# The looped turns of two attentions, written out in place of loops on the engines

## The reference

```python
def reference(...):
    x = x + _L0_attn_ref(_layernorm(x), ...)   # pre-norm attention with RoPE, then a dense FFN 128-512-128
    x = x + _L0_ffn_ref(_layernorm(x), ...)    # 16 experts, top 2, gates from a softmax, relu
    x = x + _L1_attn_ref(_layernorm(x), ...)   # causal attention, plus a bias from "lines" with decay
    x = x + _L1_ffn_ref(_layernorm(x), ...)    # 8 experts, top 2, gelu
    return x
```

## Time and profile before

| | us |
|---|---|
| median of 3 runs | 2036.21 |
| lowest, highest run | 2025.66, 2040.84 |
| the profiled execution as a run | 2023.77 |
| its span in the profile | 2022.0 |

### The profile page before, as it was taken

How to read it: one execution, slowest core, us unless ns; L and a number is a source line. 1 busy time by engine, 2 the same in 40 slices (tenths; PEclk the granted TensorE clock), 3 DMA queues, 4 the chain that set the end, 5 groups by cost and what they waited for, 6 DMA issues and landing times. The chain is left out here.

```text
span 2022.0 us, 39979 instructions
## 1 busy us (share of the span) xinstructions
PE 1540.8 (76%) x11726; PEld 971.8 (48%) x11726; DVE 1276.1 (63%) x3485; ACT 891.2 (44%) x1807; POOL 681.4 (34%) x774
## 2 busy tenths in 40 slices
PE   1699989889899861999246898798888978324993
PEld 0133433334333330999124566566665756323993
DVE  1577878777787622555515686877777867453555
ACT  0156646555455530565132555445545534102552
POOL 2211222332222213455263343334433310474552
PEclk9989989979799875899558999999999999656997
DMA  4211011110111050222324434443343340411225
GB/s 106 63 52 46 30 51 53 35 60 24 50 52 46 13 190 20 65 73 68 109 74 135 123 110 124 120 135 115 107 146 107 115 129 31 121 45 50 72 69 148
DMA packets 121565, 165.67 MB, mean 82 GB/s; under 512 B 21459, under 2 KB 94963, under 8 KB 120787
## 3 DMA queue, kind: packets, MB, share of 16 engines
q1 hardware_dynamic: 112530, 145.69, 24.4%
q0 software_dynamic: 8896, 18.30, 2.6%
HBM read 116.04 MB, written 47.60 MB: 81 GB/s over the span
## 5 line engine op out<-in xcount | busy, mean ns | idle before, releaser
L943 DVE TENSOR_REDUCE a_M<-a_F 128x1 f32<-128x512 f32 x512 | 326.1, 680 | 87.4 <-PE a_F L1115 68.3
L840 ACT ACTIVATE L_W<-a_ST 128x512 f32<-128x512 f32 x512 | 277.3, 594 | 163.7 <-PE a_ST L1155 159.7
L1738 ACT ACTIVATE c_PT<-c_ST 128x1024 f32<-128x1024 f32 x160 | 163.2, 1020 | 197.1 <-PE c_ST L2045 154.4
L1155 PE MATMUL a_ST<-L_W 74*128 74x512 bf16 x512 | 179.5, 415 | 30.1 <-ACT L_W L840 14.0
L1115 PE MATMUL a_F<-L_W 72*128 72x512 bf16 x512 | 178.6, 425 | 16.1 <-DVE a_M L943 15.7
L2044 PE MATMUL c_ST<-ident,c_SD 128*128 128x128 f32 x512 | 144.1, 281 | 26.9 <-issue 17.3
L1134 PE MATMUL a_PV<-L_W,a_V 128*32 128x512 f32 x1024 | 154.9, 681 | 1.0 <-ACT L_W L840 1.0
L1155 PEld LDWEIGHTS a_ST<-L_W 74*128 74x128 bf16 x512 | 46.1, 102 | 183.3 <-ACT L_W L840 96.2
L2269 ACT ACTIVATE L_hT<-L_P,L_W1s 128x128 f32<-128x128 f32 x316 | 90.3, 368 | 98.5 <-issue 51.3
L1845 DVE TENSOR_TENSOR c_inc<-c_INC,c_table 128x512 f32<-128x512 f32 x128 | 87.5, 684 | 50.0 <-PE c_INC L2012 41.8
L2257 POOL DMA_INDIRECT L_yd<-L_ys,L_di x79 | 86.4, 1094 | 89.4 <-issue 55.9
(11 more groups left out here) (367 smaller groups left out, 3646.0 us busy)
## 6 DMA issues: line engine op xcount, KB each, us to landing
c_QS<-c_q SPq DMA_DIRECT2D x32, 504.0 KB
c_QS<-c_rd SPq DMA_DIRECT2D x32, 378.0 KB
L_xg<-L_xd SPq DMA_DIRECT2D x150, 64.5 KB
L_W<-a_q SPq DMA_DIRECT2D x32, 288.0 KB
L_W<-a_k SPq DMA_DIRECT2D x96, 96.0 KB
c_KS<-c_k SPq DMA_DIRECT2D x96, 96.0 KB
L_W<-in_L_w SPq DMA_DIRECT2D x8, 1024.0 KB, 13.3
L_got<-L_yd SPq DMA_DIRECT2D x32, 256.0 KB, 4.4
```

The costliest lines, as they stand in the source:

```text
L840: act.activation(PT[:, j, kk, :], ST[:, kk, :], ACT.Exp).then_inc(sem(exped), 1)
L943: dve.tensor_reduce(M[:, t, h:h + 1], FB[n % BANKS][:, :], AX_X, ALU.max).then_inc(sem(maxed), 1)
L1155: pe.matmul(ST[:, kk, :], KS[0:KR0, h, kt * P:(kt + 1) * P], QS[0:KR0, h, :], start=True, stop=True).then_inc(sem(scored), 1)
L1738: act.activation(PT[:, j, :, :], ST[:, :, :], ACT.Exp).then_inc(sem(exped), 1)
```

## The change

The three loops become Python loops: the body is emitted once for every turn, with i a number. The order of the pieces in a turn, the buffers and the semaphores stay as they are.

```diff
--- before.py
+++ after.py
@@ -579,7 +579,7 @@
             before = ("projected", 1, 3)
             run(0, False, True, True, False, order_of(False, True, True, False, before))
             run(1, True, True, True, False, order_of(True, True, True, False, before))
-            with eng.Fori(2, B - 2) as i:
+            for i in range(2, B - 2):
                 run(i, True, True, True, True, order_of(True, True, True, True, before))
             run(B - 2, True, True, False, True, order_of(True, True, False, True, before))
             run(B - 1, True, False, False, True, order_of(True, False, False, True, ("ffn", -2, 0)))
@@ -1370,7 +1370,7 @@
         def turns(eng, run):
 
             run(0, False, True, True, order_of(False, True, True, (NEXT[-1][0], 1, NEXT[-1][2])))
-            with eng.Fori(1, B - 2) as i:
+            for i in range(1, B - 2):
                 run(i, True, True, True, order_of(True, True, True, ("pv", -1, NQ - 1)))
             run(B - 2, True, True, False, order_of(True, True, False, ("pv", -1, NQ - 1)))
             run(B - 1, True, False, False, order_of(True, False, False, ("pv", -1, NQ - 1)))
@@ -1611,7 +1611,7 @@
             prep(0, first=True)
             shape_table()
             prep(1)
-            with pool.Fori(2, B) as i:
+            for i in range(2, B):
                 bias_tokens(i - 2)
                 prep(i)
             bias_tokens(B - 2)
```

## The result

The changed kernel takes 2021.7 us at the median (2005.92 to 2029.05, 17 runs); beside it the kernel before took 2038.26 us (2023.01 to 2047.61, 17 runs). The ratio is 0.9929, 95% interval 0.9907 to 0.9951: 0.7% faster. That is inside the range of the prediction and within 1%, but it is a gain where 2 us of loss were forecast.

What follows compares the result with a forecast made beforehand. The prediction took looped turns to be bound by TensorE and its exchanges with ScalarE and VectorE, in the second attention also by transfers. Terms -0.3 - 1.0 + 3.0 + 0.3 = +2.0 us on 2036.2 gave 2038 us, range 2020 to 2056.

Steps and rivals of the forecast that it cites:

- Back edges: Loop ends of both attentions: hidden in the first, saving 0; four in the second at 0.08 us save 0.3 us.
- Register instructions: Semaphore targets computed in looped turns: 0.11 us each where one holds a wait, one per turn on the path, saving 1.0 us.
- Instruction fetching: Written-out turns must be fetched: turns 2 to 5 of the second attention lose 3.0 us, the first attention 0.3 us.
- The clock: First attention's turns 2 to 5: tiny shifts move the clock's falls, gain of 8 or loss of 11 us; 22 in 100.
- The faster rival: Both attentions: TensorE's waiting register instructions all on the path, 17.3 us saved, 2019 us; 9 in 100 with the other faster rival.
- The 3 in 100 for a saving of fetches at the back edges: Second faster rival, at the loops' back edges: writing out saves instruction fetches there; 3 in 100.
- The slower rival: Mainly second attention: fetches delay many awaited transfers, 0.80 us each, up to 56 us; 11 in 100.

Runs made afterwards that it cites:

- the fast place: The follow-up runs beside which the unchanged kernel before took 1989 and 1988 us, where other follow-up runs had it at 2021 to 2024 us.
- rest_out: Kernel before with the turns of all engines but TensorE written out in both attentions; ratio 0.9929 to the kernel before.
- pe_out: Kernel before with only TensorE's turns written out in both attentions, other engines looped; ratio 1.0014 to the kernel before.
- swap_loops: Kernel before, loops kept, ScalarE's two waits ahead of each exponential in exchanged order; ratio 0.9997 to the kernel before.
- more_reg: Kernel before, loops kept, one more register target and wait for ScalarE ahead of each exponential in looped turns; ratio 0.9988 to the kernel before.
- one_turn_loops: Changed kernel with each written-out turn inside a loop of one pass, entry and branch kept; ratio 0.9906 to the kernel before.
- one_turn_2: Repeat of one_turn_loops, the changed kernel with each written-out turn in a loop of one pass; ratio 0.9861 to the kernel before.
- first_only: Kernel before with only the first attention's loop written out; ratio 0.9992 to the kernel before.
- second_only: Kernel before with only the second attention's loops written out, the common one and GpSimd's own; ratio 0.9988 to the kernel before.

## Why the prediction was wrong

**Back edges (-0.3 us).** Mis-sized. The pair of the earlier trace rows compared a back edge (4.52) with a loop's entry (4.44), and both carry loop work. Against the written-out boundary of 4.20 us, the entry costs 0.24, four back edges 0.32 each and the exit 0.09: 1.6 us. The first attention's 0 was right, its last two steps keep 3.70 us in all turns.

**Register instructions (-1.0 us).** Right in kind, too small and on the wrong engine. I counted TensorE's; the runs put most of the price on the other engines, the fixed steps on ScalarE and VectorE, which stand between TensorE's results and its next operands. The fixed steps are 4 x 0.18 and 5 x 0.22, together 1.8 us. "0.11 us each, one per turn" missed that the first attention has three such places and the second three.

**Instruction fetching (+3.3 us).** This is the step that failed and turned the sign of the sum. The packets came (36 in four turns), the delay did not. I had one fetched turn, in which ScalarE waited 1.78 us before line 1671, and made it the price of every fetched turn. In the eight profiles in which all turns are written out or stand in loops of one turn, 40 turns moved 8 to 10 instruction packets each and the wait was 0.95 to 0.98 us in all of them. It was over 1 us in 12 turns of the other profiles (up to 2.64 us), ten of them turn 1, all with 8 to 10 packets; in turns without packets it was never over 0.99 us. So a fetch may still be part of that delay in some programs, and what else it takes is open. I had written "the rows show the coincidence, not the cause" and priced it nonetheless. In the changed kernel the wait was 0.96 us against 0.98, so there the term is 0.

With these corrected the sum is about -3.4 us in place of +2.0: the right sign, and a fifth of the 16.6 us measured.

**The clock (22 in 100, 2030 to 2049 us, "no cause in the edit").** This was the larger omission. I took the falls as luck that could go either way. Outside the fast place all 20 turns with VectorE and ScalarE looped had two falls, and 12 of the 24 without register instructions; in the means of three profiles turns 2 to 5 of the first attention hold a gain as large as the whole (15.5 us). From the earlier trace rows I compared turn lengths by clock only, and never asked what TensorE waited for ahead of the second fall.

**The faster rival (17.3 us on the path, 2019 us).** Its number came out nearly, but not its mechanism: the fixed costs are 3.4 us. At equal clock the gain is 7 to 13 us; the rest of it I put down to the waits of the first attention's steps 9 to 18 and the second's step 13, which are not fixed. What joins them to the register instructions is argued from correlations, not shown. The 3 in 100 for a saving of fetches at the back edges had nothing under them: in the four turns of the second attention that follow a back edge no instruction packet moved.

**The slower rival** is out: the changed kernel's five turns of the second attention took 79.5 to 83.0 us, none the 84 us that would have spoken for it.

## What to carry to other kernels

Look for register instructions that themselves hold the wait that ends last, on the engines between the critical engine's output and its next input, not on the critical engine (at equal clock rest_out gained 12.0 us, pe_out 2.5). Those whose signal had come long before cost nothing here: 60 more of them a turn of the first attention in swap_loops made +0.6 (±2.2) us. Compare a loop with straight code, not with its own entry (4.52 us against 4.20, not against 4.44). Where an exchange races with other traffic, a small change can go with a large one: here 4.60 to 4.78 us between the scatter's start and the maxima's issue went with a wait within 2.5 us in 14 of 15 turns, 4.82 to 5.13 us with one of 3.7 us or more in 11 of 14. So profile each version several times and compare means before giving a cause to one pair of traces.

## What the runs showed of the hardware

- TensorE's results came up to 3.7 us late at a full granted clock, during an indirect scatter by GpSimd, in some groups of runs and not in others. The record gives chip number 6 both to group 3 (the kernel before at 2021 us, late results) and to group 5 (1988 us, none in two profiles, whose scatter was moved), so the chip number doesn't tell the places apart. Turns 2 to 7 of the first attention, looped, took 484 us with late results (mean of three profiles) and 455 and 450 us without (swap_loops, more_reg): most of the 34 us between the places. What delays them is open, and the long wait for a_ml came twice without them.
- In the fast place the changed kernel gains 0.5% (ratio 0.9949, interval 0.9931 to 0.9967), elsewhere 0.7 to 0.9%.
- A loop of one turn, with its entry and branch in place, cost nothing that was measured here: at equal clock one_turn_loops was 2.6 us ahead of the changed kernel, one_turn_2 0.4 us behind it.
- A loop body was not fetched again in later passes, and in the changed kernel 36 packets more in four turns left ScalarE's wait before line 1671 at 0.96 us.
- What is not settled: how the register instructions come to be worth 7 to 13 us at equal clock when the fixed steps hold 3.4, and why first_only and second_only gained only 0.1% each in time while at equal clock they add up, that is, why the mean clock was higher in the changed kernel than in either half.
